# A graph attention layer's edge tiles: 127 edges in a tile instead of 128

## What is computed

```python
Qh = (x @ Wq.T + bq).reshape(n, H, D)
Kh = (x @ Wk.T + bk).reshape(n, H, D)
Vh = (x @ Wv.T + bv).reshape(n, H, D)
Ee = (edge_attr @ We.T + be).reshape(-1, H, D)
score = (Kh[src] * Qh[dst] * (1.0 / np.sqrt(D)) * Ee).sum(-1)
score = jnp.exp(jnp.clip(score, -5.0, 5.0))
msg = Vh[src] * score[..., None]
wV = jax.ops.segment_sum(msg, dst, num_segments=n)
...
x = _layernorm(x + wV)
```

## Time and profile before

| | |
|---|---|
| runs | 1814.88 and 1819.0 us, median 1816.94 |
| span of the profiled execution, first to last instruction | 1816.0 us |
| that execution's time outside the span | not listed; the median is 0.9 us above the span |
| TensorE matmuls busy | 1671.1 us, 92% |
| GpSimd busy | 1366.6 us, 75%, of which gathers 1348.7 us |
| VectorE busy | 1320.3 us, 73% |
| ScalarE busy | 968.4 us, 53% |
| DMA | 129 GB/s over the span |

### The profile page before, as it was taken

One profiled execution on the slowest core, in us unless ns is written; L12 is line 12 of the kernel. 1 busy time (PEld: TensorE's weight loads), 2 busy tenths in 40 slices (PEclk: granted clock), 3 DMA queues, 4 the chain that ended last, 5 costly groups with the idle time before them and its releaser, 6 DMA issues. The chain is left out here.

```text
span 1816.0 us, 47296 instructions
## 1 busy us (share of the span) xinstructions
PE 1671.1 (92%) x13047; PEld 1483.1 (82%) x13047; DVE 1320.3 (73%) x2197; ACT 968.4 (53%) x2864; POOL 1366.6 (75%) x1348
## 2 busy tenths in 40 slices
PE   6399999999999999999999999999999999999994
PEld 6388888888888888888888888888888888888883
DVE  6377777777777777777777777777777777777774
ACT  5355555555555555555555555555555555555553
POOL 5677777777777777777777777777777777777774
PEclk8699999999999999999999999999999999999995
DMA  7455444444444444444444444444444444444441
GB/s 234 129 139 136 127 132 126 127 126 129 130 123 124 134 129 124 128 133 127 128 133 127 122 132 130 125 125 135 127 124 125 133 129 125 123 128 132 127 114 61
DMA packets 198830, 234.44 MB, mean 129 GB/s; under 512 B 96742, under 2 KB 123180, under 8 KB 198684
## 3 DMA queue, kind: packets, MB, share of 16 engines
q1 hardware_dynamic: 156732, 147.96, 27.7%
q0 software_dynamic: 42080, 86.26, 19.5%
HBM read 226.67 MB, written 7.38 MB: 129 GB/s over the span
## 5 line engine op out<-in xcount | busy, mean ns | idle before, releaser
L258 POOL DMA_INDIRECT kv<-kv_table,idx x1315 | 1348.7, 1026 | 416.4 <-issue 402.2
L652 PE MATMUL xg_bank<-x_hi,src_onehot 128*128 128x448 f32 x2079 | 786.5, 378 | 6.7 <-DVE src_onehot L784 6.7
L653 PE MATMUL xg_bank<-x_lo,src_onehot 128*128 128x448 f32 x2079 | 759.7, 365 | 0.0
L723 ACT ACTIVATE distance<-iota_w,dst_neg 128x64 f32<-128x64 f32 x1612 | 428.4, 339 | 0.0
L652 PEld LDWEIGHTS xg_bank<-x_hi,src_onehot 128*128 128x128 f32 x2079 | 391.8, 188 | 35.3 <-DVE src_onehot L784 6.9
L653 PEld LDWEIGHTS xg_bank<-x_lo,src_onehot 128*128 128x128 f32 x2079 | 392.3, 189 | 27.3
L820 DVE TENSOR_TENSOR kq<-kv,qe_ps 128x512 f32<-128x512 f32 x202 | 138.5, 686 | 332.3 <-DMA kv<-kv_table,idx 325.6
L784 DVE TENSOR_TENSOR src_onehot<-r_row,node_of 128x896 fp32r<-128x896 f32 x297 | 322.9, 1087 | 25.0 <-DMA r_row<-r_table 25.0
L641 PE MATMUL sum_ps<-onehot,msg 128*64 128x64 f32 x3224 | 228.4, 225 | 77.6 <-DVE msg L840 77.6
L641 PEld LDWEIGHTS sum_ps<-onehot,msg 128*64 128x64 f32 x3224 | 208.8, 139 | 102.9 <-DVE msg L840 100.9
L749 ACT COPY xg_t_sb<-turn_bank 64x256 f32<-64x256 f32 x198 | 61.9, 312 | 330.6 <-PE turn_bank L663 240.8
(11 more groups left out here) (116 smaller groups left out, 1049.4 us busy)
## 6 DMA issues: line engine op xcount, KB each, us to landing
attr_sb<-attr SPq DMA_DIRECT2D x201, 256.0 KB
dst_row<-dst_rows SPq DMA_DIRECT2D x402, 128.0 KB
kv<-kv_table,idx POOLq DMA_INDIRECT x1315
r_row<-r_table SPq DMA_DIRECT2D x99, 128.0 KB, 3.1
q_win<-q_table SPq DMA_DIRECT2D x404, 24.0 KB
r_row<-r_table SPq DMA_DIRECT2D x99, 64.0 KB, 2.9
idx<-src_tab SPq DMA_DIRECT2D x206, 4.0 KB, 4.1
kv_table<-kv_stage SPq DMA_DIRECT2D x7, 448.0 KB, 3.8
```

The costliest lines, as they stand in the source:

```text
L258: pool.indirect_dma_start(out=kv[:, slot, t, :], out_offset=None, in_=kv_table, in_offset=bass.IndirectOffsetOnAxis(ap=idx[:, slot, t:t + ...
L652: pe.matmul(xg, src_onehot[:, parity, u, :], x_hi[:, u, :], start=(u == 0), stop=False)
L653: mm = pe.matmul(xg, src_onehot[:, parity, u, :], x_lo[:, u, :], start=False, stop=(u == U - 1))
L723: made = act.activation(distance[:, t, :], iota_w[:, :], ACT.Square, bias=dst_neg[:, ds(g, 1), t:t + 1].rearrange("p o t -> p (o t)"))
```

## The change

A tile now holds R = 127 edges. The edges are cut into 1625 tiles instead of 1612, 204 groups instead of 202; the last group has one pair of tiles instead of two. The arrays keep 128 places per tile; the last place repeats the 127th edge's source and destination, and its features are zero. A gather fetches 127 rows into partitions 0 to 126. Partition 127 of kv (32 partitions of it) is set to zero once, on VectorE in the first stage, and GpSimd waits for that before its first gather. The sums contract over 127 partitions; all other instructions still work on 128. PE_END stays 200, so TensorE's share is the same 297 tiles of groups 2 to 199, and groups 200 to 203 have none.

```diff
+R = 127
...
-TILES = -(-E // P)
+TILES = -(-E // R)
...
-assert ITERS * SLOTS < G <= PE_END + SLOTS and TILES % 2 == 0 and SLOTS == 4
+assert ITERS * SLOTS < G <= PE_END + SLOTS and SLOTS == 4
...
+        kv_cleared = sem("kv_cleared")
...
-                    out=kv[:, slot, t, :], out_offset=None, in_=kv_table,
-                    in_offset=bass.IndirectOffsetOnAxis(ap=idx[:, slot, t:t + 1], axis=0))\
+                    out=kv[0:R, slot, t, :], out_offset=None, in_=kv_table,
+                    in_offset=bass.IndirectOffsetOnAxis(ap=idx[0:R, slot, t:t + 1], axis=0))\
                     .then_inc(kv_gathered[slot], 16)
...
+                pool.wait_ge(kv_cleared, 1)
                 pool.wait_ge(idx_first, 16 * SLOTS)
...
+                dve.memset(kv[96:P, :, :, :], 0.0).then_inc(kv_cleared, 1)
                 base_b = base_f[:, :].unsqueeze(2).to_broadcast([P, G, T])
...
-                            mm = pe.matmul(sum_ps[0:F, slot % 2, 0:W], msg[:, slot % 2, t, :],
-                                           onehot[:, slot, t, :], start=(t == 0), stop=(t == n - 1))
+                            mm = pe.matmul(sum_ps[0:F, slot % 2, 0:W], msg[0:R, slot % 2, t, :],
+                                           onehot[0:R, slot, t, :], start=(t == 0), stop=(t == n - 1))
...
-        padded = np.full(G * T * P, fill, a.dtype)
+        padded = np.full(G * T * R, fill, a.dtype)
         padded[:E] = a
-        return padded.reshape(G, T, P)
+        tiles = padded.reshape(G, T, R)
+        return np.concatenate([tiles] + [tiles[:, :, R - 1:]] * (P - R), 2)
```

More of the change, by code:

```diff
@@ L1013 @@
     dst_rows = np.ascontiguousarray(dst_tiles.reshape(G, PAIRS, 2, P).transpose(0, 2, 1, 3)).reshape(G, 2, PAIRS * P)
-    dst_first = np.ascontiguousarray(np.broadcast_to(dst[::T * P][None, :], (P, G)))
-    attr = np.zeros((G * T * P, F), edge_attr.dtype)
-    attr[:E] = edge_attr
+    dst_first = np.ascontiguousarray(np.broadcast_to(dst[::T * R][None, :], (P, G)))
+    attr_edges = np.zeros((G * T * R, F), edge_attr.dtype)
+    attr_edges[:E] = edge_attr
+    attr = np.zeros((G, T, P, F), edge_attr.dtype)
+    attr[:, :, :R] = attr_edges.reshape(G, T, R, F)
     attr = np.ascontiguousarray(attr.reshape(G, PAIRS, 2, P, F).transpose(0, 2, 4, 1, 3)).reshape(G, 2 * F, PAIRS * P)
```

## The result

The changed kernel takes 4791.53 us (4791.30 to 4791.76, two runs) against 1816.94 us: 2.639 times the time before, interval 2.632 to 2.647. It is far slower, outside the range that was given (1740 to 1970 us).

What follows compares the result with a forecast made beforehand. GpSimd's gathers were taken as the bound, TensorE close behind. With cheaper gathers, 1816.0 less TensorE's 73.1 us of waits, +1 in the tail, gives 1744; 13 us of waits on VectorE make 1757 us, range 1740 to 1970.

Steps and rivals of the forecast that it cites:

- What bounds the kernel: Whole kernel: GpSimd's gathers set the pace at 1.3275 us each, with TensorE as the next bound.
- 4% less would have handed the bound to TensorE: Loop: a gather 0.06 us cheaper, 4% of its 1.3275 us, already makes TensorE the bound.
- The firm term: Tail on GpSimd: 14 more gathers at an unchanged 1.3275 us each add 18.6 us, fully on the path.
- The clearing of kv at 0: First stage on VectorE: a 4.2 us memset, absorbed by idle time, costs 0; at most 1.2 us without that cover.
- the sums over 127 partitions at 0: TensorE: 3254 matmuls instead of 3224, each taken at an unchanged price; 10 ns either way would be 33 us.
- cheaper by at least 0.06 us: Gathers on GpSimd: rows going to one engine spare the others' data packets, so each gather gets cheaper; chance 0.45.
- The upper bound that I set: Gathers on GpSimd: at most every gather as long as the first, 1.95 us, about 2.25 us each in place.
- The argument against the dear side: Gathers on GpSimd: they do not lengthen by what their rows are, only by what else runs.
- The rival on the other side: Gathers on GpSimd: an uneven gather costs more, +0.1 to +0.35 us each, giving 1969 to 2294 us; chance 0.33.
- Hidden in the loop, since four slots lie between: Loop: rows landing up to 4.0 us later cost nothing, as four slots separate a gather from its slot's reuse.
- The 4 us: Behind the last gather: if all its rows go to one engine, the late landing shows once, +4 us.
- All gathers on one engine: Gather queue: every gather falls on the same engine, 1329 x 4.3 us = 5.7 ms; chance 0.03.

Runs made afterwards that it cites:

- e1_rows128: The changed kernel with each gather fetching 128 rows again, everything else of the change kept: 1827.35 us, ratio 1.0069 to the kernel before.

## Why the prediction was wrong, step by step

**What bounds the kernel: right.** GpSimd's chain of gathers set the time; from the first gather to the end of the last, the time per gather went from (1790.7 - 25.4) / 1315 = 1.342 to (4762.6 - 25.2) / 1329 = 3.565 us, and the span grew as much as this chain within 2 us. That 4% less would have handed the bound to TensorE wasn't reached from this side.

**The firm term, +18.6 us for 14 more gathers: right in kind**, +12 us in e1_rows128, where the rest of the change stands.

**The clearing of kv at 0, the sums over 127 partitions at 0: right.** The memset took 3.47 us on VectorE instead of 4.2, and its cover held: VectorE still waited 3.33 us for first_i after it. The sums have the same median at the same clock, 222 ns at 1.0 over 128 and over 127 partitions. There are 3252 of them, not 3254, which changes nothing.

**The step that failed is the price of the gather: "cheaper by at least 0.06 us".** The reasoning went from true parts, sixteen engines with two packets each, to a false whole: that an engine without rows costs GpSimd less. The runs showed as many 4-byte pieces for each engine without rows as the fullest one has rows (15 x 127 of them a gather), and a gather's time that grows by 13.1 ns with each row on the fullest engine. The upper bound that I set, 1.95 us a gather, was too low as well; it was read from one long gather of 128 rows and says nothing of a gather with more in it. The argument against the dear side, that gathers do not lengthen by what their rows are, had no ground either, as all gathers of before had the same 128 rows; with 127 the median went from 944 to 2548 ns. No row of before could bound this from above, and the prediction said that nothing excluded it but priced it at +0.1 to +0.35 us; it was +1.60, over 1329 gathers more than 2100 us.

**The rival on the other side had the direction and the place, not the size.** The gather itself became dearer on GpSimd, as it said, by 1.60 us in the median. It had a chance of 0.33, and its time, 1969 to 2294, was too short by far.

**"Hidden in the loop, since four slots lie between": wrong.** The rows did land later, 4.4 us after the end of the last gather (4762.6 to 4766.96) instead of 2.1, and 4.75 us in the median by the end of the packet of 3584 bytes, so 2 to 3 us later where 4 was put, and the slots would have covered that. The 4 us took all rows of a gather as on one engine, for which no row of before spoke; the packets of the changed kernel show it. But at 199 places from the 31st gather on the next gather began only 0.59 to 0.61 us after a semaphore update of the last gather or the last but one. I looked for what reuses the slot in SBUF and not for what else can wait for a landing. This term, priced at 4 us once, is 858 us: the 861.9 us more of "issue", less 14 ordinary gaps.

**All gathers on one engine: not so.** A gather's large packets take 15 x 237 + 186 ns = 3.7 us on its engine, and 1329 of them, 4970 us, would not fit into the span of 4789.

## What to carry to other kernels

Measure the row count of a gather as a thing that has a price: of the seven counts here the two multiples of 16 are the cheapest (933 and 944 ns), one row fewer than 128 made the gather 2.7 times as long on GpSimd, and even a spare row that nobody needs (128 gathered, 127 used) is worth having: 1827.35 us against 4791.53. When a transfer becomes slower to issue or to land, the reuse of its buffer is not all that can wait for the landing: 199 waits that the profile calls "issue" ended here 0.59 to 0.61 us after a semaphore update of an earlier gather, and which semaphore the gathers counted on changed the time by up to 850 us. And where no row shows an operation, the rows of other operations do not bound it from above: the range has to say so.

## What the runs showed that was not expected

- A gather that leaves engines without rows has small packets for them, 4 bytes for each row of the fullest engine: 15 x 127 x 4 = 7620 bytes a gather for 127 rows, none for 128 or 112.
- A gather's median issue time follows the rows of the fullest engine: 933, 944, 997, 1209, 2202, 2362, 2548 ns for 7, 8, 9, 25, 101, 113, 127 rows, with a step of 40 ns between 8 and 9, where engines are first left without.
- Which semaphore a gather counts on changes the time: 4790.75, 4213.72 and 3940.76 us for one, two and three per slot, with the same gathers, data and waits for the same rows.
- The long gathers have one companion. In the kernel before, from 100 us on, all 223 gathers over 994 ns overlap VectorE's comparison of r_row with node_of (src_onehot), in the changed kernel all 191 over 2598 ns; no run takes the comparison away.
